# Two zero products per step between the gate products of a GRU kernel

## What is computed

```
x = x + einsum('bsi,io->bso', x * ys[:, None, :], weight) * d[:, None, :]     # linear layer, all steps at once
Xz, Xr, Xh = (einsum('btc,hc->tbh', x, W) + b for the three input weights)    # input projections
def step(H, (xz, xr, xh)):
    Z = sigmoid(xz + H @ Whz.T + bhz)
    R = sigmoid(xr + H @ Whr.T + bhr)
    H_tilda = tanh(xh + (R * H) @ Whh.T + bhh)
    H_new = Z * H + (1 - Z) * H_tilda
    return H_new, H_new @ Whq.T + bhq
x = x + scan(step)
```

## Time and profile before

| | |
|---|---|
| median of 3 runs | 642.17 us (641.68 to 643.65) |
| profiled execution | 641.54 us |
| its span, first to last instruction | 639.7 us |
| TensorE busy | 626.1 us, 98% of the span |
| VectorE busy | 490.9 us, 77% |
| ScalarE busy | 209.2 us, 33% |
| mean granted TensorE clock | 0.524 of full speed |

### The profile page before, as it was taken

How to read it: one execution, slowest core, us unless ns; L and a number is a source line. 1 busy time by engine, 2 the same in 40 slices (tenths; PEclk the granted TensorE clock), 3 DMA queues, 4 the chain that set the end, 5 groups by cost and what they waited for, 6 DMA issues and landing times.

```text
span 639.7 us, 39673 instructions
## 1 busy us (share of the span) xinstructions
PE 626.1 (98%) x16826; PEld 567.4 (89%) x16826; DVE 490.9 (77%) x4047; ACT 209.2 (33%) x1607; POOL 4.5 (1%) x11
## 2 busy tenths in 40 slices
PE   8999999999999999999999999999999999999986
PEld 3689999999999999999999999999999999999875
DVE  5788877777877778787777777777787777777775
ACT  3133333333333332333333333333333333333322
POOL 2000000000000000000000000000000000000000
PEclk9955555555555555555555555555555555555555
DMA  7000000000000000000000000000000000000000
GB/s 263 3 4 3 11 6 4 13 4 12 4 5 12 5 12 4 12 5 4 13 4 12 4 13 4 5 12 5 12 5 4 13 4 13 5 12 4 4 12 11
DMA packets 6629, 8.84 MB, mean 14 GB/s; under 512 B 818, under 2 KB 4914, under 8 KB 6452
## 3 DMA queue, kind: packets, MB, share of 16 engines
q1 hardware_dynamic: 5872, 6.03, 2.9%
q10 hardware_dynamic: 580, 0.28, 0.2%
HBM read 4.21 MB, written 2.10 MB: 10 GB/s over the span
## 4 chain that ended last, share of the span: by engine, by line
PE 93%; DVE 4%; ACT 1%; DMA 1%; issue 1%; DVEq 0%
PE chunk_bank L625 53%; PE z_rec_bank L625 13%; PE chunk_bank L617 12%; PE z_bank L617 6%; PE y_bank L602 6%; PE chunk_bank L634 1%; DMA x<-x_cm 1%; PE chunk_bank L554 1%; DVE lin L367 1%; PE y_bank L560 1%; DVE r_hidden L490 1%; DVE hidden L534 1%; DVE r_hidden L494 0%; DVE r_hidden L498 0%; ACT scan_mul L316 0%
## 5 line engine op out<-in xcount | busy, mean ns | idle before, releaser
L625 PE MATMUL chunk_bank<-r_hidden,w_part 128*128 128x8 bf16 x6144 | 206.3, 169 | 0.2
L625 PEld LDWEIGHTS chunk_bank<-r_hidden,w_part 128*128 128x128 bf16 x6144 | 184.8, 105 | 18.3 <-issue 0.6
L625 PEld LDWEIGHTS chunk_bank<-hidden,w_part 128*128 128x128 bf16 x3072 | 102.4, 104 | 36.0 <-DVE hidden L534 7.4
L625 PE MATMUL chunk_bank<-hidden,w_part 128*128 128x8 bf16 x3072 | 125.0, 173 | 6.2 <-DVE hidden L534 6.2
L534 DVE TENSOR_TENSOR_SCAN hidden<-scan_mul,hidden 128x24 f32<-128x24 f32 x512 | 80.5, 199 | 60.6 <-ACT hidden L319 54.3
L316 ACT ACTIVATE scan_mul<-z_pre 128x16 f32<-128x16 f32 x256 | 57.2, 223 | 197.2 <-DVE z_pre L502 197.2
L625 PE MATMUL z_rec_bank<-hidden_parts,w_part 128*128 128x24 bf16 x3072 | 121.5, 181 | 0.1
L625 PE MATMUL chunk_bank<-hidden_parts,w_part 128*128 128x8 bf16 x3072 | 119.2, 168 | 0.0
L314 ACT ACTIVATE r_bank<-chunk_bank 128x8 f32<-128x8 f32 x256 | 41.5, 162 | 212.1 <-PE chunk_bank L625 206.6
L625 PEld LDWEIGHTS z_rec_bank<-hidden_parts,w_part 128*128 128x128 bf16 x3072 | 103.2, 104 | 0.2 <-DVE z_rec_bank L449 0.2
L625 PEld LDWEIGHTS chunk_bank<-hidden_parts,w_part 128*128 128x128 bf16 x3072 | 102.9, 104 | 0.0
(11 more groups left out here) (80 smaller groups left out, 656.8 us busy)
## 6 DMA issues: line engine op xcount, KB each, us to landing
x<-x_cm SPq DMA_DIRECT2D x4, 512.0 KB, 8.1
out_cm<-result SPq DMA_DIRECT2D x16, 128.0 KB, 2.1
w_rec<-w_rec_cm SPq DMA_DIRECT2D x1, 768.0 KB, 8.4
w_in<-w_in_cm SPq DMA_DIRECT2D x1, 768.0 KB, 9.9
w_mod<-w_mod_cm ACTq DMA_DIRECT2D x1, 256.0 KB, 5.5
w_out<-w_out_cm SPq DMA_DIRECT2D x1, 256.0 KB, 10.4
cond<-cond_cm ACTq DMA_DIRECT2D x1, 8.0 KB, 1.7
bias_rows<-gate_bias ACTq DMA_DIRECT2D x1, 4.0 KB
```

The costliest lines, as they stand in the source:

```text
L625: return nc.tensor.matmul(cols, w_part[wp][:, gate, k, m * P:(m + 1) * P], moving, start=first, stop=True, skip_group_check=True)
```

## The change

A function `fill` issues one bf16 product of zeros by zeros with a given number of columns, and adds it to columns 384 and up of a PSUM bank that nothing reads there. The loop calls it twice per step: with 46 columns behind the first bulk product, ahead of gate G, and with 74 columns behind the other five, ahead of the next step's gate R. In the first and the last block it does nothing. So 14 blocks of 16 steps get two products each, 448 in all. Each needs a weight load of 128 columns of zeros. No wait and no semaphore is added, and what the other engines run is as before.

```
+            FILL_AHEAD_OF_R, FILL_AHEAD_OF_G = 74, 46
+
+            def fill(n, j, cols):
+
+                if n == 0 or n == NB - 1:
+                    return
+                bank = y_bank if j < 4 else z_bank if j < 8 else chunk_bank[1 - n % 2][j % 4 // KC]
+                nc.tensor.matmul(bank[:, 3 * BC:3 * BC + cols], zeros[:, 0:P], zeros[:, 0:cols],
+                                 start=False, stop=True, skip_group_check=True)
...
                 bulk(n, j, slice(0, 1))
+                fill(n, j, FILL_AHEAD_OF_G)
...
                 gate_products(G, t, p, j, rh_parts, rh_ready, (r_ready[1], t + 1), rh_rest, rh_rest2, pre_g)
...
                 bulk(n, j, slice(1, len(PRODUCTS)))
+                fill(n, j, FILL_AHEAD_OF_R)
```

## The result

| | before | after |
|---|---|---|
| median of 10 runs | 642.36 us (640.38 to 643.77) | 645.47 us (644.32 to 647.37) |
| ratio to before, 95% interval | | 1.0046 (1.0033 to 1.0059) |
| span of the profiled execution | 639.7 us | 642.6 us |
| mean granted TensorE clock | 0.524 | 0.526 |
| period of a step in the steady stretch | 2.373 us | 2.385 us |

The changed kernel is slower by a little under half a per cent. The clock is where it was; a step has become 12 ns longer.

A forecast was written before the change was run, and what follows sets the result against it. The round trip of gates R and G to the scan was taken as the bound; 220 steps x 15 ns plus 0.25 us for fp32 steps gave 645.7 us. Its own range was 643.0 to 647.5, eight in ten 634.5 to 648.5.

The forecast's parts named there:

- What bounds a step: Steady steps: the round trip gate R to scan sets 2.373 us; bulk products lie in its holes.
- Ahead of gate G, cost 0: Ahead of gate G: the 38 ns fill fits a hole of about 60 ns, at no cost.
- Ahead of gate R, a hole of 40 ns read by ends: Ahead of gate R: the 62 ns fill is 20 ns too long for a hole of about 40 ns.
- Three quarters of a delay arrive: Gate R's lateness: three quarters reaches the step, so 20 ns late cost 15 ns per step.
- The fp32 steps of block 1 pay the whole 62 ns: Block 1's four fp32 steps: gate R already follows the tile, so 62 ns come in full, 0.25 us.
- Its signs: What would show the forecast, including four steps at 40 to 67 us growing by 62 ns each.
- The sum: Whole kernel at 1.2 GHz: 220 steps x 15 ns plus 0.25 us, giving 645.7 us, +0.5%; chance 42%.
- its price: Worth of the upper TensorE clock: 32 ns per step, 7.0 us over 220 steps.
- The rival that it rises: TensorE's clock rises to 2.4 GHz and stays, both fills fit: 635.4 us, -1.1%; chance 34%.
- it rises at times: TensorE's clock rises at times, other steps pay 15 ns: between 637 and 644 us; chance 6%.
- the hole ahead of gate R is 60 ns: Ahead of gate R the fill just fits, only the fp32 steps pay: 642.4 us; chance 12%.
- the zeros' load or the hand-over is exposed: At each fill 28 ns more, making 42 ns per step, 9.2 us: 651.6 us; chance 6%.

The follow-up runs named there:

- g_only: Changed kernel with only the 46 columns of zeros ahead of gate G, none ahead of gate R; ratio 0.9991 to the kernel before.
- swapped: Changed kernel with the two sizes exchanged, 74 columns ahead of gate G and 46 ahead of gate R; ratio 0.9983 to the kernel before.
- packed: Against hold: gate Z's products and the first twelve of gates R and G stream their columns twice, zeros refitted; 633.44 us, ratio 0.9842 to the kernel before.
- r_only: Changed kernel with only the 74 columns of zeros ahead of gate R, none ahead of gate G; ratio 1.0040 to the kernel before.
- r_twice: Changed kernel with the 74-column product ahead of gate R issued twice; ratio 1.0278 to the kernel before.
- hold: Every block's steps get 128-column products of zeros, one ahead of gate G (none in the first step), four or eight ahead of R; ratio 1.154 to kernel before.
- hold_more: hold with more 128-column products of zeros: two ahead of gate G, five or ten ahead of gate R; ratio 1.236 to the kernel before.

## Why the prediction was right

**What bounds a step: right.** The round trip of gate R, sigmoid, multiply, gate G, tanh and scan sets it, and products beside it are free as far as they fit. g_only and swapped add 46 and 120 columns per step for nothing; packed adds over a thousand at 2.4 GHz, and its period is the 2.34 us of the very first steps.

**Ahead of gate G, cost 0: right.** 0.9991 for that product alone.

**Ahead of gate R, a hole of 40 ns read by ends: right.** r_only carries the loss, swapped takes it away, and in the rows after the gate's first product ends right behind the zeros. The gate's first product ends 0.47 us after its scan's start there (300.40 to 300.87) against 0.45 before; over all steps from 80 to 598 us it is 0.475 against 0.455: the 20 ns.

**Three quarters of a delay arrive: mis-sized.** It gave 15 ns per step; the period grew by 2.385 - 2.373 = 12 ns, and the ratios give 12 (8 to 16), with r_only 11 (7 to 14). So 15 is at the upper edge, and these two alone would hardly refute it. r_twice does: there nearly all of the delay arrives, so it is not a share. A first part of about 8 ns that is swallowed fits these runs, and the fp32 steps from which the three quarters came as well (45 ns late, 34 paid, with rows that step by 10 ns). What exactly swallows it was argued (later waits of the same gate for the split state), not shown.

**The fp32 steps of block 1 pay the whole 62 ns: right, but not where the prediction looked for them.** Its signs name four steps at 40 to 67 us. That stretch is block 0, which has no zeros, and its steps are as long as before (2.40 us against 2.41). Block 1 begins about where it ends. There the scans were 2.41 us apart before, and after 2.47:

```profile
66.33 0.32 DVE L534 TENSOR_TENSOR_SCAN hidden<-scan_mul,hidden 128x24 f32<-128x24 f32 x2 [0.36 <-ACT hidden L319]
68.73 0.32 DVE L534 TENSOR_TENSOR_SCAN hidden<-scan_mul,hidden 128x24 f32<-128x24 f32 x2 [0.36 <-ACT hidden L319]
71.14 0.32 DVE L534 TENSOR_TENSOR_SCAN hidden<-scan_mul,hidden 128x24 f32<-128x24 f32 x2 [0.36 <-ACT hidden L319]
...
66.42 0.32 DVE L534 TENSOR_TENSOR_SCAN hidden<-scan_mul,hidden 128x24 f32<-128x24 f32 x2 [0.37 <-ACT hidden L319]
68.89 0.32 DVE L534 TENSOR_TENSOR_SCAN hidden<-scan_mul,hidden 128x24 f32<-128x24 f32 x2 [0.36 <-ACT hidden L319]
71.36 0.32 DVE L534 TENSOR_TENSOR_SCAN hidden<-scan_mul,hidden 128x24 f32<-128x24 f32 x2 [0.36 <-ACT hidden L319]
73.82 0.32 DVE L534 TENSOR_TENSOR_SCAN hidden<-scan_mul,hidden 128x24 f32<-128x24 f32 x2 [0.36 <-ACT hidden L319]
```

**The sum.** 220 x 15 ns + 0.25 us was 3.5 us; with 12 ns it is 2.9, which is what the spans differ by (642.6 - 639.7). The medians of ten runs differ by 3.1. The forecast of 645.7 us was 0.2 over the measured 645.47, and that close it came by luck: it stood on a median before of 642.17 us, which was 642.36 in the ten runs. Measured by the difference it was 3.5 against 3.1 (2.1 to 3.8 by the interval of the ratio).

**The clock: it did not rise, and its price was right.** The rival that it rises had 34%, that it rises at times 6%; no stretch from 70 to 605 us is above 0.50. Kernels with five and more times as many columns of zeros did not raise it either (hold, hold_more). What it would be worth, 32 ns per step, is what packed shows: 2.373 - 2.340 = 33 ns. The Trainium skill (TensorE: Matmul & The Clock Gate, "Why this matters for your kernels") asks for TensorE to be kept busy continuously. In the prologue of packed that and the rows agree: the clock came back under an unbroken row of fp32 products of 512 columns. In the steps they differ, and the rows decide: after the change there was a record for every nanosecond from 70 to 605 us, and the clock stood at 0.50; it came back during the steps in none of the kernels here that had lost it.

**The other rivals.** That the hole ahead of gate R is 60 ns (12%) is refuted by r_only and swapped. That the zeros' load or the hand-over is exposed (6%, 651.6 us) is refuted by g_only and by the rows after, where gate R's first product ends 10 ns behind the zeros (300.86 to 300.87), about its own 8 columns.

## What to carry to other kernels

Measure a hole between two matmul records by their ends: a record can start while its product still stands behind another, and here the starts gave 60 and 40 ns for holes of 40 and 60. Before filling a hole ask what waits behind it, and compare the fill with the hole at the clock that is granted now, not at the one hoped for. If the upper clock is wanted, try to keep the one that a dense prologue has from the very first sparse step on, with real width in the small products whose starts are no closer for being narrow, and look at the granted clock over the whole run; in this kernel, once lost in the steps, it did not come back before they ended in any run.

## What the runs showed of the hardware

- In the steps the clock went down without any long pause of TensorE: in the kernel before at 30.1 us, after steps whose longest idle time was 0.41 us, in hold and hold_more with no idle time at all between 26.8 us and the fall.
- It did not come back at 1.2 GHz in over 700 us of nearly unbroken products (hold: 640 columns of zeros and 1440 others in each step of 2.774 us with a bulk tile), while packed, with 2560 columns in 2.340 us, kept it to the end. The same products of zeros that were free at 2.4 GHz (periods of 2.34 us in the first steps of both) cost 15% in hold and 24% in hold_more at 1.2.
- It did come back elsewhere: in the prologue of packed under fp32 products of 512 columns, and in hold_more behind the last step (0.95 over 790.00 to 793.80 us), after ten products of zeros and while the last eight fp32 products ran.
- A pair of weight load and product takes 27 ns at 1.2 GHz and 25 at 2.4 with 8 columns; 16 columns at 2.4 GHz took no longer (twelve in 0.49 us against 0.48). So the upper clock gains a chain of small products little by itself, and 33 ns of a 2.37 us step in all.
